# Packed transposes of the attention weights, and a new order on VectorE, in a cross-attention and mixture-of-experts kernel

## The reference

```python
x = x + attention(layernorm(x), ctx, ctx, mask) # softmax over the 77 context rows, then Wo
x = x + ffn(layernorm(x))
# ffn: top-1 of 16 experts (gate, up, down of width 512), scaled by sigmoid of its logit,
#      plus a shared expert: silu(x @ w_gate.T) * (x @ w_up.T) @ w_down.T
```

## Time and profile before

| what | value |
| --- | --- |
| time, median of 3 runs | 390.08 us (389.37 to 391.12) |
| profiled execution, its own time | 387.37 us |
| its span, first to last instruction | 385.7 us |
| mean granted PE clock | 0.987 |
| PE busy | 349.3 us, 91% |
| DVE busy | 191.4 us, 50% |
| ACT busy | 172.8 us, 45% |
| POOL busy | 159.6 us, 41% |

### The profile page before, as it was taken

One profiled execution on the slowest core, in us unless ns is written; L12 is line 12 of the kernel. 1 busy time (PEld: TensorE's weight loads), 2 busy tenths in 40 slices (PEclk: granted clock), 3 DMA queues, 4 the chain that ended last, 5 costly groups with the idle time before them and its releaser, 6 DMA issues.

```text
span 385.7 us, 9343 instructions
## 1 busy us (share of the span) xinstructions
PE 349.3 (91%) x3068; PEld 224.6 (58%) x3068; DVE 191.4 (50%) x567; ACT 172.8 (45%) x472; POOL 159.6 (41%) x271
## 2 busy tenths in 40 slices
PE   3858898999999999998999999979998999999990
PEld 2545666777777777776776888433444344444440
DVE  2589899967958849767742761211212121212110
ACT  2278969665574655656642302222333333323320
POOL 6266656423522623423221011353464646474531
PEclk9999999999999999999999999998999999999996
DMA  7510102020089200000014999385457888698600
GB/s 216 216 45 3 45 9 64 14 59 2 28 280 397 103 0 27 27 18 12 27 38 144 401 262 406 108 301 215 127 195 270 265 309 276 226 315 316 218 14 21
DMA packets 23614, 58.04 MB, mean 151 GB/s; under 512 B 7307, under 2 KB 14493, under 8 KB 20128
## 3 DMA queue, kind: packets, MB, share of 16 engines
q1 hardware_dynamic: 16992, 50.16, 37.0%
q0 software_dynamic: 2880, 6.31, 4.9%
q10 hardware_dynamic: 3712, 1.22, 1.4%
HBM read 149.94 MB, written 6.82 MB: 406 GB/s over the span
## 4 chain that ended last, share of the span: by engine, by line
PE 31%; issue 27%; POOL 16%; DVE 14%; ACT 5%; DMA 4%; POOLq 1%; DVEq 0%; ACTq 0%
PE ps L668 8%; POOL xs L521 5%; POOL attT L529 5%; PE ps L674 5%; PE ps L595 4%; PE ps L610 3%; DMA rows<-score 3%; POOL pool_carrier L510 3%; POOL out L536 3%; PE ps L649 2%; DVE arena L1154 2%; PE ps L620 2%; ACT arena L962 2%; DVE den L1163 2%; PE ps L635 2%
## 5 line engine op out<-in xcount | busy, mean ns | idle before, releaser
L468 POOL TENSOR_TENSOR arena<-arena,rden 128x308 f32<-128x308 f32 x64 | 44.7, 700 | 93.9 <-DVE rden L1167 93.2
L962 ACT ACTIVATE arena<-arena,negtop 128x77 f32<-128x77 f32 x256 | 70.6, 350 | 19.2 <-DVE negtop L1159 19.2
L1383 DVE TENSOR_TENSOR act_g<-act_g,ps 128x512 f32<-128x512 f32 x20 | 13.7, 687 | 88.1 <-PE ps L884 74.2
L510 POOL TENSOR_TENSOR pool_carrier<-neghalf 1x1 f32<-1x1 f32 x60 | 11.0, 183 | 76.7 <-DVE qT L1390 43.8
L620 PE MATMUL ps<-ident,arena 128*77 128x128 f32 x256 | 39.8, 280 | 2.7 <-ACT arena L970 2.7
L884 PE MATMUL ps<-own,qT 128*32 128x512 f32 x320 | 38.1, 618 | 4.3 <-DMA own<-w_experts 3.4
L668 PE MATMUL ps<-xn2T,w_gu 128*128 (+1 forms) x160 | 39.5, 390 | 0.6 <-ACT xn2T L975 0.6
L620 PEld LDWEIGHTS ps<-ident,arena 128*77 128x77 f32 x256 | 29.2, 147 | 11.1 <-issue 7.1
L668 PEld LDWEIGHTS ps<-xn2T,w_gu 128*128 128x128 f32 x160 | 28.8, 190 | 10.0 <-issue 5.9
L884 PE MATMUL ps<-arena,qT 128*32 128x512 f32 x288 | 32.8, 595 | 0.7 <-DMA arena<-w_experts 0.5
L1062 ACT ACTIVATE qT<-ps 128x256 f32<-128x256 f32 x20 | 7.7, 383 | 54.6 <-PE ps L868 54.6
(11 more groups left out here) (157 smaller groups left out, 572.4 us busy)
## 6 DMA issues: line engine op xcount, KB each, us to landing
own<-w_experts SPq DMA_DIRECT2D x44, 1024.0 KB
arena<-w_experts SPq DMA_DIRECT2D x40, 1024.0 KB
own<-w_experts SPq DMA_DIRECT2D x44, 512.0 KB
arena<-w_experts SPq DMA_DIRECT2D x40, 512.0 KB
arena<-x SPq DMA_DIRECT2D x8, 256.0 KB, 3.1
xn2T<-w_experts SPq DMA_DIRECT2D x2, 1024.0 KB, 6.2
x<-w_experts SPq DMA_DIRECT2D x4, 512.0 KB, 7.2
rows<-xn_now SPq DMA_DIRECT2D x7, 256.0 KB, 2.6
```

Source lines behind the costliest of these rows:

```text
L468: pool.tensor_tensor(prob[k][:, :, :], prob[k][:, :, :], rden[k][:, :].rearrange("p (h o) -> p h o", o=1).to_broadcast([P, HU, K]), ALU.mu ...
L962: ins = act.activation(prob[k][:, h, :], prob[k][:, h, :], ACT.Exp, bias=negtop[k][:, h:h + 1])
```

## The change

- The 616 exponentials of two units stand side by side in `pair`, padded to 640 = 5 x 128 columns (`NCH` = 5). Transposes take blocks of 128 columns whatever the head: two for the even unit, three for the odd one, where there were four each. ACT copies 128 x 256 and 128 x 384 in place of 77 x 512 twice.
- A pair of heads then lies across two blocks. The values must stand on the matching partitions, so `vz` is 128 partitions, five blocks. `place_values` leaves POOL for SP: twelve DMAs a batch, of rows of 16 numbers, between on-chip buffers. `attend_pair` still issues eight products.
- DVE goes by pairs of units: both masks, both tops, then both sums and both inversions of the pair before. The last `early_hidden` stands right behind the sums of the last pair; it, the second norm, the key and value reads, and `add_early` are put in new places.
- The first norms of batches 2 and 3 are taken in passes 0 and 1, in place of passes 1 and 2; that of batch 1 moves behind pass 0's first pair.
- `project_q` moves to step 6 in passes 3 to 6 and to step 5 in passes 0 to 2; `transpose_xn` to step 3 in passes 0 to 2. ACT and POOL follow.

```diff
@@ -122,24 +123,28 @@
-        val = sb("val", [K, D])
-        vz = [carve(H * HG, K).rearrange("k (h d) -> k h d", h=H) for s in range(2)]
-        prob = [carve(HU * K).rearrange("p (h k) -> p h k", h=HU) for s in range(UB)]
+        val = [sb(f"val{s}", [K, D]) for s in range(2)]
+        vz = [carve(DC * NCH * P).rearrange("p (c j d) -> p c j d", c=DC, j=NCH) for s in range(2)]
+        pair = [carve(NCH * P) for s in range(UB // 2)]
+        prob = [pair[s // 2][:, (s % 2) * HU * K:(s % 2 + 1) * HU * K].rearrange("p (h k) -> p h k", h=HU) for s in range(UB)]
...
-        probT = [(carve(HU * P, K) if s < 4 else spread[0:K, (s - 4) * HU * P:(s - 3) * HU * P]).rearrange("k (h n) -> k h n", h=HU) for s in range(UB)]
+        probT = [(carve(NCH * P) if s < UB // 4 else spread[:, (s - UB // 4) * NCH * P:(s - UB // 4 + 1) * NCH * P]).rearrange("p (j n) -> p j n", j=NCH)
+                 for s in range(UB // 2)]
@@ -246,6 +252,14 @@
+        pieces = []
+        for h in range(HC):
+            r = h * K
+            while r < (h + 1) * K:
+                end = min((h + 1) * K, (r // P + 1) * P)
+                pieces.append((h, r - h * K, r // P, r % P, end - r))
+                r = end
@@ -288,6 +302,18 @@
+            def place_values(b):
...
+                s = b % 2
+                sp.wait_ge(val_ready, b + 1)
+                if b == 0:
+                    sp.wait_ge(vz_zero, 2)
+                if b >= 2:
+                    sp.wait_ge(pv_done, UB // 2 * (b - 1))
+                for h, k, j, p, n in pieces:
+                    sp.dma_start(vz[s][p:p + n, :, j, h * HD:(h + 1) * HD],
+                                 val[s][k:k + n, :].rearrange("k (c d) -> k c d", c=DC)[:, :, h * HD:(h + 1) * HD]).then_inc(vals_in[s], 16)
@@ -298,6 +324,7 @@
+                place_values(b)
@@ -315,7 +342,10 @@
-                if 1 <= g <= 3:
+                if g in (1, 2):
+                    store_rows(sp, g + 2)
+                    place_values(g + 5)
+                if g == 3:
                     store_rows(sp, g + 2)
@@ -419,9 +448,10 @@
+            for a in range(UB // 2):
+                pool.memset(pair[a][:, PAIR:NCH * P], 0.0).then_inc(pad_zero, 1)
...
-                pool.memset(vz[s][:, :, :], 0.0).then_inc(vz_zero, 1)
-            pool.wait_ge(zero_ready, 1)
+                pool.memset(vz[s][:, :, :, :], 0.0).then_inc(vz_zero, 1)
@@ -451,18 +481,6 @@
-            def place_values(q, s, n):
...
-                b = 2 * q + s
-                pool.wait_ge(val_ready, b + 1)
-                if n in (0, 1):
-                    pool.wait_ge(vz_zero, 2)
-                else:
-                    pool.wait_ge(pv_done, UB // 2 * (b - 1))
-                pairs = lambda a: a.rearrange("k (p a d) -> k p a d", a=2, d=HD)
-                pool.tensor_tensor(vz[s][:, :, :].rearrange("k (p a) (b d) -> k p (a b) d", a=2, b=2)[:, :, 0:4:3, :],
-                                   pairs(val[:, :]), pairs(zeros[0:K, :]), ALU.add).then_inc(vals_ready, 1)
@@ -472,22 +490,20 @@
             def batch(q, s, n):
...
-                    if k == 0 and n != B - 1:
-                        rstd_first(nq, ns)
...
-                    if k == 2 and n not in (0, 1):
+                    if k == 5 and n not in (0, 1):
                         rstd_second(q - 1, s)
...
-                    if k == 1 and n == 0:
-                        place_values(0, 0, 0)
+                    if k == 1 and (n is None or n == 0 or n >= EARLY):
+                        rstd_first(nq, ns)
+                    if k == 5 and n in (0, 1):
+                        rstd_first(q + 1, s)
...
-                    if k == UB - 1:
-                        place_values(nq, ns, None if n is None else n + 1)
@@ -612,12 +628,16 @@
             def transpose_prob(q, s, k, started):
...
+                if not started and k == 1:
+                    pe.wait_ge(pad_zero, UB // 2)
...
-                for h in range(HU):
-                    mm = pe.transpose(ps[0:K, bank_pt[k % 2], h * P:(h + 1) * P], prob[k][:, h, :], ident[:, :])
+                for j in (range(2, NCH) if k % 2 else range(2)):
+                    mm = pe.transpose(ps[:, bank_pt[k % 2], (j % 2 if j < 2 else j - 2) * P:(j % 2 + 1 if j < 2 else j - 1) * P],
+                                      pair[k // 2][:, j * P:(j + 1) * P], ident[:, :])
@@ -626,15 +646,14 @@
                 if k == 0:
-                    pe.wait_ge(vals_ready, b + 1)
+                    pe.wait_ge(vals_in[s], 16 * len(pieces) * (q + 1))
...
-                    for j in range(HC // 2):
-                        h = 2 * j + a
-                        mm = pe.matmul(ps[HG * j:HG * (j + 1), bank_o, c * S + t * P:c * S + (t + 1) * P],
-                                       vz[s][:, c * HC + h, :], probT[k + h // HU][:, h % HU, :],
-                                       start=(a == 0), stop=(a == 1))
+                    for g in range(HC // 2):
+                        j = HG // HD * g * K // P + a
+                        mm = pe.matmul(ps[HG * g:HG * (g + 1), bank_o, c * S + t * P:c * S + (t + 1) * P],
+                                       vz[s][:, c, j, HG * g:HG * (g + 1)], probT[k // 2][:, j, :], start=(a == 0), stop=(a == 1))
@@ -687,7 +706,7 @@
-                        pe.wait_ge(q_out, DC * (b + 2))
+                        pe.wait_ge(val_ready, b + 2)
@@ -704,6 +723,9 @@
+                    if k == 6 and shared and not last:
+                        pe.wait_ge(early_h, FC * (2 * q + (s - EARLY)) + 3)
+                        project_q(nq, ns, bank_m[0])
@@ -723,11 +745,11 @@
-                    if k == 2 and not last:
+                    if k == (2 if shared else 3) and not last:
                         if n not in (0, 1):
...
-                    if k == 3 and not last:
+                    if k == 5 and not last and not shared:
                         project_q(nq, ns, bank_m[0])
@@ -967,7 +989,8 @@
-                act.activation(probT[k][:, :, :].rearrange("p h n -> p (h n)"), ps[0:K, bank_pt[k % 2], :],
+                lo, hi = (2, NCH) if k % 2 else (0, 2)
+                act.activation(probT[k // 2][:, lo:hi, :].rearrange("p j n -> p (j n)"), ps[:, bank_pt[k % 2], 0:(hi - lo) * P],
@@ -986,6 +1009,9 @@
+                    if not shared and k % 2 == 0 and (k >= T_LAG or n != 0):
+                        read_probT(*unit_at(q, s, k - T_LAG), n not in (0, 1) or (n == 1 and k >= T_LAG))
+                    exponential(q, s, k)
@@ -993,16 +1019,17 @@
-                    exponential(q, s, k)
+                    if k == 6 and shared and n != B - 1:
+                        read_q(nq, ns, bank_m[0])
...
-                    if k >= T_LAG or n != 0:
+                    if (shared or k % 2) and (k >= T_LAG or n != 0):
                         read_probT(*unit_at(q, s, k - T_LAG), n not in (0, 1) or (n == 1 and k >= T_LAG))
-                    if k == 2 and n != B - 1:
+                    if k == (2 if shared else 3) and n != B - 1:
                         read_xnT(nq, ns)
...
-                    if k == 3 and n != B - 1:
+                    if k == 5 and not shared:
                         read_q(nq, ns, bank_m[0])
@@ -1150,7 +1178,7 @@
-                    dve.wait_ge(pt_psum, u - 7)
+                    dve.wait_ge(pt_psum, u - 7 + (1 - k % 2))
@@ -1173,6 +1201,9 @@
+            def ln2_stats(q, s):
+                b = 2 * q + s
@@ -1217,44 +1248,56 @@
-                for k in range(UB):
-                    if k == 0 and not last:
-                        ln1_stats(nq, ns)
-                    if k >= S_LAG or n != 0:
-                        sum_prob(*unit_at(q, s, k - S_LAG))
-                    mask_scores(q, s, k, n != 0)
-                    if k >= S_LAG or n != 0:
-                        invert(*unit_at(q, s, k - S_LAG))
-                    find_top(q, s, k)
-                    if k == 0 and n == 0:
+                for j in range(UB // 2):
+                    both = (2 * j, 2 * j + 1)
+                    for k in both:
+                        mask_scores(q, s, k, n != 0)
+                    for k in both:
+                        find_top(q, s, k)
+                    if j > 0 or n != 0:
+                        for k in both:
+                            sum_prob(*unit_at(q, s, k - S_LAG))
+                        for k in both:
+                            invert(*unit_at(q, s, k - S_LAG))
+                    if j == 0 and n == 0:
                         dve.wait_ge(kv_psum, 1)
...
-                        read_v(bank_f, 0)
-                    if k == 0 and not last:
+                        read_v(0, bank_f, 0)
+                    if j == 0 and not shared:
+                        read_kv(nq, ns)
+                    if j == 0 and not last and (shared or n == 0):
+                        ln1_stats(nq, ns)
+                    if j == 0 and n not in (0, 1):
+                        add_attention(q - 1, s)
+                    if j == 0 and not last and (shared or n == 0):
```

(48 more changed lines are left out.)

24 lines of the change are left out of this document (14 added, 10 removed).

## The result

On one chip, four runs each, the changed kernel takes 385.17 us (382.18 to 385.80), the kernel before 389.73 us (388.09 to 391.12). The ratio is 0.989, interval 0.985 to 0.993: 4.6 us faster, about half of the 8.7 us of the forecast; 385.17 lies inside the range of 377.0 to 387.0.

What follows compares the result with a forecast made beforehand. PE's instruction count was taken to pace passes 3 to 6, DVE passes 1 and 2. Passes 3 to 6 -8.0, pass 7 -1.4, tail -0.3, start and passes 0 to 2 +1.0: -8.7, giving 381.4 us; range 377.0 to 387.0.

Steps and rivals of the forecast that it cites:

- 32 x 0.129 less 20 x 0.108: Transposes of each pass: fewer, packed ones save PE 1.97 us, taken as 2.0, lower bound 1.3.
- The cover of the fourth gated product: Passes 3 to 6: PE's other work covers the chain to the down products, slack 0.3 us, no wait counted.
- A: A ring of waits, DVE to ACT to DVE to PE, paces passes at 26.2 us; total 386.1 us; chance 0.17.
- C: Passes 3 to 7: down products wait for the fourth gated product, making it slower, 393.6 us; chance 0.07.
- Rival D: Transposes' pace follows their loaded columns, so packing gains only the short waits; about 389.9 us; chance 0.04.
- Values by DMA: Twelve copies a batch on SP's queue, 0.47 us each to issue, 8 to 17 us in all, hidden, cost nothing.
- (a): Start: POOL clears more columns, so DVE's apply starts later; +0.75 us on everything behind.
- (d): Pass 2: DVE asks for keys and values before PE has them, a wait of about 2.2 us.
- (b): Start: batch 1's first norm leaves DVE's idle time before the first mask; +1.85 us.
- (c): Norms taken ahead move 1.85 us from pass 2 to pass 0; no change to the sum.
- (e): Start and passes 0 to 2: DVE's waits for exponentials, up to 3.6 us, can go; counted as -3.6.
- Start that much earlier: Routing and routed experts: untouched, so they only start earlier by the time gained before them; no change of their own.

Runs made afterwards that it cites:

- fourth_late: Changed kernel with the fourth gated product moved behind the second norm's last step and the mask read on DVE; 391.23 us, ratio 1.008.
- not_ahead: Changed kernel with the first norms of batches 2 and 3 put back to passes 1 and 2; 396.60 us, ratio 1.002.
- resid_later: Changed kernel with POOL's residual addition moved from step 2 to step 6; 381.53 us, ratio 0.982.
- resid_5: Changed kernel with POOL's residual addition at step 5 instead of step 2; 386.56 us, ratio 0.978 on a slower chip.
- warm_early: Changed kernel with dummy transposes of the identity added where PE waits in passes 0 and 2; 381.56 us, ratio 0.982.

## Why the prediction was right or wrong

**The direction held, and 385.17 us lies in the range**, but the gain was 4.6 us in place of 8.7: passes 3 to 7 gave what the forecast had, and the early passes and the routed experts took back 4 us by the medians, 6 by the traces. Point by point:

*Passes 3 to 6: right sum, wrong terms.* The step "32 x 0.129 less 20 x 0.108" was mis-sized. The transposes of a pair of units took 1.03 us and take 0.69, so four pairs give 1.36 us, and the runs 1.33, where I had 1.97. The rows after say why: three transposes last 0.49 us, 0.108 from one to the next, but the scores behind them start 0.42 after the group's start. The 0.129 of the earlier trace rows was a group with the step to the scores in it, the 0.108 one without; both shapes go at 0.11, as the earlier trace rows had it: four of either take 0.60 us, at 127.39 and at 127.82. Packing saves 12 instructions at 0.11, my lower bound of 1.3. The other 0.70 us a pass came from the orders, which I had at nothing: PE's idle time of 0.35 went, with the wait of 0.22 in it, and its busy time fell from 26.84 to 26.48, for which I have no cause. The two errors cancelled to 2.0: that the passes came out to 0.2 us was luck.

*The cover of the fourth gated product: right*, no wait ahead of the down products in passes 3 to 6, and 0.94 us in pass 7 where I had 1.5. That this slack carries the gain is shown by `fourth_late`. Rivals A and C name this mechanism; it decides packing alone and the late product, and not the changed kernel.

*`attend_pair` over 128 partitions: right*, still 0.57 to 0.58 us for 16. *Rival D*, loads priced by columns, is dead: 0.108 us from one transpose of 128 columns to the next, as with 77.

*Values by DMA: right to be hidden*, but dearer to issue: twelve take 10.2 us on SP's queue, 0.85 each and not 0.47, and 12.7 in one batch. PE never waits for them.

```profile
118.14 10.21 SPq L315 DMA_DIRECT2D arena<-val  x12
```

*Passes 0 to 2: wrong, and this is the first half of the miss.* (a) cost 0.47. (d) was there, 2.31 us, but VectorE had that time to spare: 0.3 us. (b) and (c) were reckoned as VectorE time moved from one pass to another; what counts is whether a mask stands behind it, and the trace of `not_ahead` shows 1.6 to 4.5 us for it. The step that failed is (e): the waits for exponentials did go (3.6 to 0), and I let them count in full. They came back as waits for scores. The groups of VectorE up to the border of passes 2 and 3, the masks' row:

```profile
L1182 DVE TENSOR_TENSOR arena<-ps,spread 128x308 f32<-128x308 f32 x26 | 11.1, 470 | 9.0 <-PE ps L626 8.8
```

It was 3.8 us before. PE in turn waited for POOL, 5.5 us, which I had written off as having time anyway: with both inversions at once, its residual stands between two scalings. That wait is no rival of mine, and `resid_later` and `resid_5` show it.

*The clock.* I reckoned all durations at full clock. In the changed kernel PE waits 3.68, 0.86 and 1.29 us in pass 0, and then products run at half pace for some 5 us; L611 in pass 2 loses 1.5 us after a wait of 1.45. Both traces of the changed kernel and `warm_early` show it, and added work cured it. But in the same trace of the changed kernel pass 1 has the same wait, and L611 behind it takes 1.99 us:

```profile
42.81 0.55 PE L639 MATMUL ps<-ident,arena 128*128 128x128 f32 x3 [1.45 <-POOL arena L486]
...
44.01 1.99 PE L611 MATMUL ps<-spread,arena 128*128 128x256 f32 x8
```

Which wait brings a fall in which execution is open: the same pass of the same order came out at 18.91, 18.88 and 17.29 us.

*Routed experts: wrong, the second half.* "Start that much earlier" holds for the start (5.4 us). The weights of the second step do not come that much earlier: from SP's issue of their loads to the product that waits for them it takes 9.6 us in the kernel before and with the orders alone (248.93 to 258.53, 249.60 to 259.23), and 10.4 to 10.5 us with the changed kernel, its repeat, packing alone and `fourth_late`. So 0.8 us of longer wait comes with the packing half of the change and its copies, not with the orders; I had costed both at nothing here. By what way they delay these loads wasn't tried and stays open. The step behind that wait adds 1.0 us: 3.64 us at full clock, 5.34 before, 6.38 in the profiled execution, though 5.34 again in the repeat, so this part is of one execution. About 1 us more is longer waits for weights in later steps. In six traces with this routed code on the first two groups' chips and the result's the part takes 141.3 to 143.9 us, and with the orders alone 142.9, where the one trace before has 140.9; only the 0.8 is the same in all six. The half pace was there in the kernel before too, so the price of the wait stood in its trace and I had not read it:

```profile
258.53 5.34 PE L884 MATMUL ps<-own,qT 128*32 128x512 f32 x32 [2.42 <-DMA own<-w_experts]
```

## What to carry to other kernels

Where one engine sets the pace, less work for it counts only if what feeds it has slack at the same places: packing gave 0.24 us a pass alone and 1.33 with the orders that keep PE fed. Price a group of short instructions between two groups of the same kind; a group's quotient with the step to the next kind in it is not the instruction's. When two results that used to come one by one come as a pair, look at every engine behind them for an operation that stood between, and count a wait of microseconds on PE at possibly more than its length, for the products behind it can run at half clock. Where an edit's effect is the size of the spread between executions, price it by the stretch of the trace that it touches, and repeat the unedited kernel beside it.

## What the hardware showed that was not expected

Added work made the kernel faster: 52 transposes of a constant in waits of pass 0 and 16 in pass 2 took the ratio from 0.989 to 0.982 on one chip, and 40 in pass 0 with 20 in the routed experts from 0.978 to 0.971 on another, by keeping products at 1.99 us that else took up to 3.78, and at 3.64 that else took up to 6.52.

VectorE's norm instructions (two of 128x256) take 0.73 us alone and 1.59 or 2.16 us beside GpSimd's, by which operation runs there; masks (447 to 480 ns, all 64) and reductions (444 to 466 ns, all 128) show no such spread. One instruction's durations over the changed kernel, in ns, least, median and most:

```profile
L1145 DVE TENSOR_SCALAR arena<-arena,mv,rstd x16: 404/411/883, 7.7 to 148.5; 128x256 f32<-128x256 f32 x16
```

Small copies within the chip's memory take their queue 0.85 us each to issue, and up to 1.13 (13.5 us for twelve in one batch of `not_ahead`), where most loads for a batch on the same queue take 0.33 to 0.47.
